# Fused cross-attention and mixture-of-experts kernel: order of the max-row copies, loads, second-normalisation transposes, router and row statistics within the attention steps

## The reference, cut to what matters

```python
x = x + tanh(g_xattn[0]) * xattn(layernorm(x), ctx, ctx, mask, Wq, bq, Wk, bk, Wv, bv)
x = x + tanh(g_ffn[0]) * ffn(layernorm(x), Wg, W1, W2, W3)

def xattn(q, k, v, mask, ...):              # 64 batches, 128 tokens, 256 channels, 16 heads of 16
    scores = einsum('bqhd,bkhd->bhqk', q @ Wq + bq, k @ Wk + bk) / sqrt(10.0)
    probs = softmax(where(mask == 0, -1e9, scores))
    return einsum('bhqk,bkhd->bqhd', probs, v @ Wv + bv)

def ffn(x, Wg, W1, W2, W3):                 # 8192 tokens, 8 experts, hidden size 512
    scores = (x_flat @ Wg.T).T              # the router
    top_vals, token_idx = top_k(scores, 1024)        # each expert takes its 1024 tokens
    h = silu(xg @ W1.T) * (xg @ W3.T)       # xg = x_flat[token_idx]
    y = (h @ W2.T) * softmax(top_vals)
    return zeros.at[token_idx].add(y)
```

## Time and profile before

| | |
|---|---|
| median of 3 runs | 867.6 us (865.45 to 868.92) |
| profiled execution | 866.8 us |
| its span, first to last instruction | 865.1 us |
| PE busy | 757.8 us (88%) |
| DVE busy | 556.9 us (64%) |
| ACT busy | 512.0 us (59%) |
| POOL busy | 375.3 us (43%) |
| mean granted clock of TensorE | 0.947 of full speed |

### The profile page before, as it was taken

The page is one execution under the profiler, slowest core; times in us unless marked ns, Lnnn a source line. Parts: engine busy times, 40 slices in busy tenths (PEclk is TensorE's granted clock), DMA queues, the critical chain, the costliest instruction groups (busy, mean ns, idle before and its releaser), DMA issues. The chain is left out here.

```text
span 865.1 us, 24848 instructions
## 1 busy us (share of the span) xinstructions
PE 757.8 (88%) x9570; PEld 634.3 (73%) x9570; DVE 556.9 (64%) x1421; ACT 512.0 (59%) x1004; POOL 375.3 (43%) x793
## 2 busy tenths in 40 slices
PE   1699999999999999999998721599999999999993
PEld 1577788878887888878886510379888888888983
DVE  4367777787777777777767549754746556474440
ACT  3235577766766677767756637265555655556641
POOL 6231444534354344424422430436474654747505
PEclk9889999999999999999999955599999999999997
DMA  4423342444434452444322242135354453624314
GB/s 133 136 89 127 131 156 98 152 157 163 146 122 151 154 178 88 160 162 164 103 102 72 83 138 83 48 126 118 99 104 117 81 113 73 130 45 85 38 13 49
DMA packets 76772, 97.06 MB, mean 112 GB/s; under 512 B 8264, under 2 KB 55880, under 8 KB 76616
## 3 DMA queue, kind: packets, MB, share of 16 engines
q1 hardware_dynamic: 64368, 78.44, 26.7%
q0 software_dynamic: 12288, 17.05, 12.0%
HBM read 52.37 MB, written 25.72 MB: 90 GB/s over the span
## 5 line engine op out<-in xcount | busy, mean ns | idle before, releaser
L676 DVE TENSOR_REDUCE m_sb<-a_ps 128x4 f32<-128x512 f32 x256 | 164.5, 684 | 70.7 <-PE a_ps L905 60.1
L538 ACT ACTIVATE p_t<-b_ps 128x512 f32<-128x512 f32 x256 | 143.6, 588 | 61.1 <-PE b_ps L913 60.9
L905 PE MATMUL a_ps<-k_st,q_st 31*128 31x128 f32 x2048 | 151.0, 285 | 21.6 <-ACT p_t L538 11.4
L905 PEld LDWEIGHTS a_ps<-k_st,q_st 31*128 31x128 f32 x2048 | 127.2, 188 | 47.7 <-issue 37.0
L913 PE MATMUL b_ps<-q_st,k_st 32*128 32x128 f32 x2048 | 149.1, 283 | 1.2 <-ACT p_t L538 1.0
L1223 POOL DMA_INDIRECT out<-y,idx_add x64 | 100.3, 1567 | 110.8 <-ACT y L1282 100.0
L458 POOL TENSOR_TENSOR x<-o_n,x_res 128x256 f32<-128x256 f32 x64 | 47.0, 734 | 194.9 <-DVE o_n L761 171.6
L913 PEld LDWEIGHTS b_ps<-q_st,k_st 32*128 32x128 f32 x2048 | 124.5, 186 | 2.2 <-issue 1.4
L1592 PE MATMUL bank<-x_hi,w_hi 128*128 128x512 f32 x254 | 100.1, 394 | 0.0
L1592 PE MATMUL bank<-x_lo,w_hi 128*128 128x512 f32 x254 | 99.0, 390 | 0.0
L1592 PE MATMUL bank<-x_hi,w_lo 128*128 128x512 f32 x254 | 98.9, 389 | 0.0
(11 more groups left out here) (238 smaller groups left out, 1713.9 us busy)
## 6 DMA issues: line engine op xcount, KB each, us to landing
w<-in_w_t SPq DMA_DIRECT2D x24, 512.0 KB, 4.8
rows_scratch<-xg SPq DMA_DIRECT2D x16, 528.0 KB, 3.0
x_in<-in_x SPq DMA_DIRECT2D x16, 512.0 KB, 4.9
c_t<-in_ctx_t SPq DMA_DIRECT2D x16, 512.0 KB, 5.8
k_st<-k_val SPq DMA_DIRECT2D x64, 128.0 KB
q_st<-q_val SPq DMA_DIRECT2D x64, 128.0 KB, 2.1
x_res<-in_x SPq DMA_DIRECT2D x16, 512.0 KB, 3.8
out<-x SPq DMA_DIRECT2D x16, 512.0 KB, 6.4
```

What stands on the lines that cost most here:

```text
L538: act.activation(p_t[b.s % 2][:, 4 * r:4 * r + 4, :], b_ps[q % 2][:].rearrange("p (h s) -> p h s", s=P), ACT.Exp, scale=SCALE).then_inc(ex ...
L676: dve.tensor_reduce(m_sb[b.s % 2][:, 4 * q:4 * q + 4], a_ps[q % 2][:].rearrange("p (h s) -> p h s", s=P), AX_X, ALU.max).then_inc(max_done, 1)
L905: mm = pe.matmul(a_ps[i][:, t * P:(t + 1) * P], q_st[p][r:r + A_K, t, tok], k_st[p][r:r + A_K, t, tok], start=True, stop=True)
```

## The change

SyncE: `max_rows` becomes the first call of every step. `load_x`, `load_c` and `load_mask` leave step 0; they are issued in steps 2 and 3, for the group three ahead in place of two (at the start one load for group 2 stands in group 0's step 0). `store_x2` stands behind `stack_k`, `store_rows` moves from step 3 to step 2, behind `stack_q`.

TensorE: `xn2_back` for the first half of the channels moves from step 0 to step 3 of the step group before, for the second half from step 1 to step 0. `router` moves from step 2 to step 1, `scores_back` from step 2 to step 1, both within their half. The wait of `values` on `xt2_out` and that of `max_t` on `st_out` move with them, one step earlier.

ScalarE: `xt2_copy` moves from the end of steps 0 and 1 to the place right behind `exp 1`; `router_out` to step 1; `normalise2` for tiles 0 and 1 to the end of step 1, for tiles 2 and 3 ahead of `pv_copy` in step 3; `context_hi` from step 1 to step 0; the four `normalise` calls stand together.

VectorE: the statistics of `x_in` are split over steps 0 and 1; `score_ends` and `row_scores` move from step 2 to step 1.

Nothing is added or removed: each engine issues as many matrix products, copies and DMAs as before.

```diff
--- before.py
+++ after.py
@@ -377,20 +377,23 @@
 
             def step(sp, b):
                 g = b.group
+                max_rows(b.back(1))
                 if b.j == 0:
+                    if first(g):
+                        load_c(g.on(2))
+                        load_x(g.on(2))
+                        load_mask(g.on(2))
                     residual(g)
-                    load_x(g.on(2))
-                    load_c(g.on(2))
-                    load_mask(g.on(2))
-                if b.j == 1:
-                    store_x2(g.on(-2))
-                if b.j == 3:
-                    store_rows(g.on(-3))
-                max_rows(b.back(1))
                 if b.j == 1:
                     stack_k(g.on(1))
+                    store_x2(g.on(-2))
                 if b.j == 2:
                     stack_q(g.on(1))
+                    store_rows(g.on(-3))
+                    load_x(g.on(3))
+                if b.j == 3:
+                    load_c(g.on(3))
+                    load_mask(g.on(3))
 
             steps(sp, step)
             sp.wait_ge(r_out, NG)
@@ -589,32 +592,30 @@
                 exp(b.back(2), 0)
                 negate(b.back(1))
                 exp(b.back(2), 1)
+                if b.j < 2:
+                    xt2_copy(g.on(-3), b.j)
                 if b.j == 0:
                     if first(g):
                         xn_t_out(f, 0)
                     xn_t_out(f, 1)
                 if b.j == 2:
                     q_out(f, 1)
-                pv_copy(b.back(3))
-                if b.j == 2:
-                    router_out(g.on(-3))
-                    normalise2(g.on(-2), (0, 1))
                 if b.j == 3:
                     normalise2(g.on(-2), (2, 3))
+                pv_copy(b.back(3))
+                if b.j == 1:
+                    router_out(g.on(-3))
                 exp(b.back(2), 2)
                 exp(b.back(2), 3)
+                if b.j == 0:
+                    context_hi(g.on(2))
                 if b.j == 1:
                     q_out(f, 0)
+                    normalise2(g.on(-2), (0, 1))
                 if b.j == 2:
-                    normalise(g.on(2), (0, 1))
-                if b.j == 1:
-                    context_hi(g.on(2))
+                    normalise(g.on(2), range(GB))
                 if b.j == 3:
                     xn_t_out(g.on(2), 0)
-                if b.j < 2:
-                    xt2_copy(g.on(-3), b.j)
-                if b.j == 2:
-                    normalise(g.on(2), (2, 3))
 
             steps(act, step)
             act.wait_ge(s_const, CUTS)
@@ -814,8 +815,9 @@
                 maximum(b, 3)
                 if b.j == 0:
                     make_k(f, 0)
+                    stats(b.group.on(2), (0, 1))
                 if b.j == 1:
-                    stats(b.group.on(2), range(GB))
+                    stats(b.group.on(2), (2, 3))
                 if b.j == 2:
                     make_v(f, 0)
                 if b.j == 3:
@@ -828,13 +830,13 @@
                         fold(0, NG // GB - 1, u)
                     for u in range(2):
                         fold(NG // GB - 1, NG // GB, u)
-                if b.j == 2:
+                if b.j == 1:
                     score_ends(b.group.on(-3))
-                    if at_last(b, NG + 2, 2):
+                    if at_last(b, NG + 2, 1):
                         all_ends()
                     row_scores(b.group.on(-3))
                 for u in range(2, GB):
-                    if at_last(b, NG - 1 + u, 2):
+                    if at_last(b, NG - 1 + u, 1):
                         fold(NG // GB - 1, NG // GB, u)
 
             steps(dve, step)
@@ -919,8 +921,8 @@
                 if not b.ok:
                     return
                 if q == 0:
-                    if b.j > 1 and back.ok:
-                        pe.wait_ge(xt2_out, back.times(2, b.j - 1))
+                    if b.j in (1, 2) and back.ok:
+                        pe.wait_ge(xt2_out, back.times(2, b.j))
                     pe.wait_ge(f_free[1], b.group.times(4, 4))
                     pe.wait_ge(f_free[0], b.group.times(4, 4))
                     wait(pe, pv_out, b.times(1))
@@ -974,7 +976,7 @@
                 if use.ok:
                     if use.k + use.s == 0:
                         pe.wait_ge(f_free[1], 4)
-                    if b.j == 3 and g.ok:
+                    if b.j == 2 and g.ok:
                         pe.wait_ge(st_out, g.times(1, 1))
                     wait(pe, neg_done, use.times(1))
                     pe.wait_ge(max_done, use.times(4, 4))
@@ -1015,14 +1017,16 @@
                 front(g.on(1), 2 * b.j + 1)
                 for q in range(4):
                     values(b.back(3), q, g.on(-3))
-                if b.j == 2:
+                if b.j == 1:
                     router(g.on(-3), b)
                 scores(b, 1)
                 front(*((g.on(1), 2 * b.j + 2) if b.j < 3 else (g.on(2), 0)))
                 out_back(b)
-                if b.j < 2:
-                    xn2_back(g.on(-3), b.j, b)
-                if b.j == 2:
+                if b.j == 3:
+                    xn2_back(g.on(-2), 0, b)
+                if b.j == 0:
+                    xn2_back(g.on(-3), 1, b)
+                if b.j == 1:
                     scores_back(g.on(-3), b)
                 if at_last(b, NG, 3):
                     turns()
```

## The result

The changed kernel takes 884.36 us (median of 4 runs, 880.78 to 886.3) against 867.75 us (4 runs) before: a ratio of 1.0189 with a 95% interval of 1.0167 to 1.0211, 16.6 us slower. The profiled execution has a span of 884.6 us against 865.1. It is the slowest of the four runs, so its 19.5 us of difference are more than the medians'. The four times follow TensorE's mean granted clock over the run: 0.934 in the profiled one (886.3 us), 0.939 in the next two (884.27 and 884.45), 0.948 in the fastest (880.78).

A forecast was written before the change was run, and what follows sets the result against it. TensorE, nearly always busy and in order, was taken as the bound. Full groups 6.9 + 1.0, drain 4.7, group 2 -0.5 give +12.1 us: 879.7 us forecast, range 872 to 887 (8 times in 10).

The forecast's parts named there:

- the drain: Groups 15 and 16: four short halves lengthened by the wait for the copy; forecast +4.7 us, between 3 and 7.
- the terms of the full groups: Groups 3 to 13: 11 x 0.63 = 6.9 us longer; own range +0.45 to +0.90 per group.
- The main term: TensorE's `values` wait for ScalarE's copy out of `pv_ps`, behind two exponentials: 1.28 us in step 0, 0.31 in step 1.
- The sum per group: Groups 3 to 13, each: +1.28 +0.31 -0.43 -0.13 -0.40 = +0.63 us.
- Group 14: The group without late maxima to win back: forecast +1.03 us.
- The transposes in step 3: Four transposes fit TensorE's 0.63 us idle time in step 3's second half, which shortens from 2.82 us by 0.13.
- rival C: Further waits: step 3's maxima late (0.3 a group), VectorE's work delaying maxima (0.3), or clock falling (0.02); 887 us, chance 0.07.
- The maxima ahead of loads: Issuing maxima before loads removes TensorE's wait ahead of step 1: 0.29 us in group 6, 0.40 per group.
- Rival A: Faster: idle times are recovered and `values` in steps 0 and 1 do not wait for the copy; 861.6 us, chance 0.06.

## Why the prediction was right

The direction, the mechanism and the range held (872 to 887, measured 884.36; forecast 879.7). That the range held is in part luck: the drain alone left its own bounds (3 to 7 us), and the total stayed inside because the terms of the full groups came out in the middle of theirs.

The main term, `values` waiting for the copy. Forecast 1.28 us in step 0 and 0.31 in step 1; the rows show 1.18 and 0.25 of idle time, and by starts `values` came 3.00 us after the opening where 3.03 was forecast. The half grew by 1.25. For step 1 the starts give 3.02 where 3.03 was forecast. The sum per group was forecast as +0.63, measured 28.64 less 28.01 = +0.63. The experiments show it as a cause: with the copies moved away the loss is gone, and with the copy one slot later it grows by one slot. Group 14 was forecast as +1.03 and took 0.98 more (28.58 less 27.60). `router` costs step 1 what it gives back in step 2, 0.43 and 0.42, as forecast.

The transposes in step 3: forecast 2.69, measured 2.69 in most groups. In group 3 this half was 2.78, in groups 7 and 8 it was 2.84, and the opening behind it had 0.15 and twice 0.21 us of idle time without a releaser. Maxima that land late, the first part of rival C, would look like this, at a half of its price and in three groups of eleven. It was not told apart from the stacked keys and queries, for which the same block waits; both come by DMA.

The maxima ahead of loads: the size, 0.40 per group, was right where the edit stands alone (28.01 to 27.61). It was worked out from group 14 as one without loads; the trace has one there too, `x_res` at 428.81, 2.91 us ahead of the maxima, so the wait goes with the three loads that follow `x_res`. But as a term of this sum it was credited to the wrong part. The kernel without the new DMA order is as long as with it. The 0.40 would have been won back by the wait in step 0 alone, which lets the maxima land; the sum came out right because that gain exists either way, once.

The drain is the term that was mis-sized: +4.7 forecast, at most 7, and +11.6 in the profiled run (some 9 by the medians: 16.6 less 6.9 and 1.0 of the full groups). The four waits cost 5.4 us with the clock held, near the forecast. The rest is the clock, which the prediction had as a rival (part of C, chance 0.02), but for the full groups, where it did not fall; that the drain, with less work and four longer waits, is where it could fall I had not seen. With the clock held the kernel took 879.5 us, 12 above the kernel before, as in the forecast's +12.1.

Rival A, that the idle times are recovered and the wait is not paid, is what happens when the copies stand ahead of `exp 0`: 855.05 us. It lost on ScalarE's order, as argued. I had priced it at 861.6, since I left 0.5 per group for `xn_hi` in it; with the copies in idle slots TensorE's halves show no such cost.

## What to carry to other kernels

When an item that fills a shared bank is moved forward by one step, the reader that empties it must move forward too, to a slot that ends before the bank's next writer is due; look for the slot by the time at which the emptying engine can start it, not by its idle share. Here two placements of the same two copies, one behind two exponentials and one ahead of them, are 29 us apart. Two waits in a ring of engines need not add: in this kernel the wait for the copy hid the late landing of the same step's maxima, while the waits for the two copies, a step apart, did add. So price an edit with the other edits in place, and look at the clock in stretches where the work thins out before you call the waits there their own length.

## What the runs showed of the hardware that was not expected

The granted clock fell from 1.00 to 0.64 on the mean of 490 to 508 us, in a drain with waits of 1.6 us, and was 1.00 from 464 to 508 us when five small products that nobody reads were put into each of four waits; this made the kernel 4.9 us faster (884.36 to 879.5, medians). Ten per wait held it too, but overran the wait by 0.5 us each. The level of the clock is not the same from run to run: the changed kernel's four runs have means of 0.934 to 0.948 and times of 886.3 to 880.78 us.
